# Attention softmax transposed on VectorE in 32x32 blocks and exchanged by DMA, the value product placed behind the next scores

## The reference

```python
x = _rmsnorm(hidden_states, ln_weight)
h_q = (x @ w_q.T).reshape(b, lq, H, DH)
h_k = (key_value_states @ w_k.T).reshape(b, lk, H, DH)
h_v = (key_value_states @ w_v.T).reshape(b, lk, H, DH)
score = jnp.einsum('bqhd,bkhd->bhqk', h_q, h_k)
score = score + position_bias[None]
score = jnp.where(m, score, -jnp.inf)
score = jax.nn.softmax(score, axis=-1)
score = jnp.where(m, score, 0.0)
attn = jnp.einsum('bhqk,bkhd->bqhd', score, h_v).reshape(b, lq, H * DH)
out = attn @ w_out.T
return hidden_states + out
```

## Time and profile before

| what | value |
|---|---|
| median of three runs | 943.55 us |
| the profiled execution, first to last instruction | 942.7 us |
| PE busy | 933.8 us, 99% |
| PE weight loading busy | 816.1 us, 87% |
| DVE busy | 629.9 us, 67% |
| ACT busy | 409.5 us, 43% |
| POOL busy | 520.2 us, 55% |
| DMA, mean of 16 engines | 51.6% of the span, 182 GB/s |
| TensorE clock granted | 1.00 of full speed |

### The profile page before, as it was taken

The page is one execution under the profiler, slowest core; times in us unless marked ns, Lnnn a source line. Parts: engine busy times, 40 slices in busy tenths (PEclk is TensorE's granted clock), DMA queues, the critical chain, the costliest instruction groups (busy, mean ns, idle before and its releaser), DMA issues.

```text
span 942.7 us, 16961 instructions
## 1 busy us (share of the span) xinstructions
PE 933.8 (99%) x5517; PEld 816.1 (87%) x5517; DVE 629.9 (67%) x1161; ACT 409.5 (43%) x1143; POOL 520.2 (55%) x582
## 2 busy tenths in 40 slices
PE   9999999999999999999999999999999999999997
PEld 7888898888888888888888888988898888878885
DVE  5666664466766576756766676657665767886787
ACT  5664434344343434333434344334434344335664
POOL 3450724457565756584757565856567553133477
PEclk9999999999999999999999999999999999999999
DMA  9315327674667365745676376637673666230101
GB/s 329 110 55 177 121 116 267 215 254 153 227 228 264 119 256 197 280 150 207 221 268 204 137 268 240 212 133 279 217 271 133 224 207 224 69 123 1 35 23 68
DMA packets 61291, 171.70 MB, mean 182 GB/s; under 512 B 6056, under 2 KB 8492, under 8 KB 60989
## 3 DMA queue, kind: packets, MB, share of 16 engines
q1 hardware_dynamic: 61244, 171.11, 51.6%
HBM read 159.56 MB, written 11.53 MB: 181 GB/s over the span
## 4 chain that ended last, share of the span: by engine, by line
PE 94%; DVE 2%; ACT 1%; issue 1%; POOL 1%; DMA 1%; SPq 0%; ACTq 0%; DVEq 0%; POOLq 0%
PE ps_q L355 7%; PE ps_q L357 7%; PE ps_q L356 7%; PE ps_o L355 6%; PE ps_o L357 6%; PE ps_o L356 6%; PE ps_k L355 6%; PE ps_k L357 6%; PE ps_v L355 6%; PE ps_k L356 6%; PE ps_v L357 6%; PE ps_t L2183 6%; PE ps_v L356 6%; PE ps_s L2156 6%; PE ps_t L2173 3%
## 5 line engine op out<-in xcount | busy, mean ns | idle before, releaser
L780 ACT ACTIVATE scores<-scores,neg_max 128x128 f32<-128x128 f32 x256 | 99.8, 391 | 219.9 <-DVE neg_max L1583 219.8
L1470 DVE TENSOR_TENSOR acc<-ps_o,acc 128x512 f32<-128x512 f32 x128 | 87.8, 686 | 60.9 <-PE ps_o L357 60.9
L355 PE MATMUL ps_o<-wo_hi,att_hi 128*128 128x512 f32 x256 | 105.9, 414 | 0.0
L357 PE MATMUL ps_o<-wo_hi,att_lo 128*128 128x512 f32 x256 | 100.3, 392 | 0.0
L356 PE MATMUL ps_o<-wo_lo,att_hi 128*128 128x512 f32 x256 | 100.0, 390 | 0.0
L786 ACT COPY probs_t<-ps_t 128x512 f32<-128x512 f32 x64 | 37.7, 588 | 139.5 <-PE ps_t L2173 139.4
L1104 POOL TENSOR_TENSOR shift<-bias_sb,mask_sb 128x512 f32<-128x512 f32 x64 | 84.8, 1326 | 2.9 <-DVE scores L1579 2.9
L1458 DVE TENSOR_TENSOR att_lo<-ps_t,att_hi 128x512 fp32r<-128x512 f32 x64 | 44.2, 691 | 55.2 <-ACT att_hi L773 55.2
L1145 POOL TENSOR_TENSOR wq_lo<-raw_q,wq_hi 128x256 fp32r<-128x256 f32 x65 | 48.1, 740 | 58.9 <-ACT wq_hi L612 58.9
L355 PE MATMUL ps_v<-wv_hi,ct_hi 128*128 128x256 f32 x264 | 75.1, 284 | 0.4 <-POOL wv_lo L1125 0.3
L357 PE MATMUL ps_v<-wv_hi,ct_lo 128*128 128x256 f32 x264 | 74.7, 283 | 0.0
(11 more groups left out here) (394 smaller groups left out, 2780.9 us busy)
## 6 DMA issues: line engine op xcount, KB each, us to landing
ring_hi<-scratch_x_t SPq DMA_DIRECT2D x39, 512.0 KB, 4.0
ring_lo<-scratch_x_t SPq DMA_DIRECT2D x39, 512.0 KB, 4.9
ring_hi<-scratch_c_t SPq DMA_DIRECT2D x39, 512.0 KB, 4.0
ring_lo<-scratch_c_t SPq DMA_DIRECT2D x39, 512.0 KB, 5.3
raw_o<-in_w_o SPq DMA_DIRECT2D x16, 512.0 KB, 4.9
raw_q<-in_w_q SPq DMA_DIRECT2D x15, 512.0 KB, 6.4
raw_k<-in_w_k SPq DMA_DIRECT2D x15, 512.0 KB, 7.1
xt_hi<-scratch_x_t SPq DMA_DIRECT2D x13, 512.0 KB, 7.3
```

The source lines that it names most:

```text
L355: pe.matmul(dst, hi_l, hi_r, start=first, stop=False)
L357: return pe.matmul(dst, lo_l, hi_r, start=False, stop=last)
L780: e = act.activation(probs[n][:, m, :], scores[n][:, m, :], ACT.Exp, bias=neg_max[:, n, m:m + 1], accum_out=row_sum[:, n, m:m + 1])
L1470: dve.tensor_tensor(acc[:, b, :], ps_o[:], acc[:, b, :], ALU.add).then_inc(o_added, 1)
```

## The change

The transposition leaves PE. Where a score tile is q by k, DVE now writes the sum of score and bias in another order: column k = 4r + j of tile m goes to place (j, m, r). Exponentials and division work on this order. Then one DVE instruction transposes all 32x32 blocks of the 128x512 tile in place. After it, partition 32i + r holds for each j and m the 32 query rows of block i at key 4r + j. Four DMAs, issued by ACT (pt_exchange), bring these to probs_t: DMA i takes 32 partitions with four pieces of 512 bytes each and writes 128 partitions, one piece to each. PE reads probs_t as four runs of 32 columns for a product with the values. The last step, 63, keeps the old way over PE and ACT.

The value product of a step moves behind the scores of the next step, and the split into low part moves on DVE behind the next softmax_front. The number of projection units between the value product and output part 0 becomes two; for that, one unit moves ahead of output part 0 in c = 0, 1, 2 and 3. The exponentials no longer wait for the transposes of two steps before; softmax_front waits until the exchange of two steps before has landed.

```diff
+Q = 32
...
+        def by_block(tile):
+
+            return tile[:].rearrange("p a b -> p (a b)").rearrange("p (j m r) -> p j m r", j=4, m=4)
+
+        def flat(tile):
+            return tile[:].rearrange("p a b -> p (a b)")
...
+        pt_in, PT_ALL = pt_out, 64 * (STEPS - 1)
...
             def exponentials(s, n):
 
                 act.wait_ge(s_neg, s + 1)
-                wait_from(act, pt_done, s - 1)
                 for m in range(4):
-                    e = act.activation(probs[n][:, m, :], scores[n][:, m, :], ACT.Exp,
+                    tile = scores[n][:, m, :] if isinstance(s, int) and s == STEPS - 1 else by_block(scores[n])[:, :, m, :]
+                    e = act.activation(tile, tile, ACT.Exp,
                                        bias=neg_max[:, n, m:m + 1], accum_out=row_sum[:, n, m:m + 1])
                 e.then_inc(e_done, 1)
 
+            def pt_exchange(s, n):
+
+
+
+                act.wait_ge(p_done, s + 1)
+                for i in range(4):
+                    act.dma_start(probs_t[:, i, :], scores[n][i * Q:(i + 1) * Q, :, :]).then_inc(pt_in, 16)
+
             def pt_evac(s):
-                act.wait_ge(pt_done, s + 1)
+                act.wait_ge(pt_done, 1)
...
-                pt_evac(s)
+                pt_exchange(s, n)
...
-                dve.tensor_tensor(scores[n][:], blocks(ps_s), shift[n][:], ALU.add).then_inc(s_shifted, 1)
-                dve.wait_ge(s_shifted, s + 1)
-                dve.tensor_reduce(row_max[:, n, :], scores[n][:], AX_X, ALU.max).then_inc(s_chain, 1)
-                dve.wait_ge(s_chain, 3 * s + 1)
+                wait_from(dve, pt_in, 64 * (s - 1))
+                if isinstance(s, int) and s == STEPS - 1:
+                    dve.tensor_tensor(scores[n][:], blocks(ps_s), shift[n][:], ALU.add).then_inc(s_shifted, 1)
+                    dve.wait_ge(s_shifted, s + 1)
+                    dve.tensor_reduce(row_max[:, n, :], scores[n][:], AX_X, ALU.max).then_inc(s_chain, 1)
+                else:
+                    dve.tensor_tensor(by_block(scores[n]).rearrange("p j m r -> p m r j"),
+                                      ps_s[:].rearrange("p (m r j) -> p m r j", m=4, j=4),
+                                      shift[n][:].rearrange("p m (r j) -> p m r j", j=4), ALU.add).then_inc(s_shifted, 1)
+                    dve.wait_ge(s_shifted, s + 1)
+                    dve.tensor_reduce(row_max[:, n, :], by_block(scores[n]).rearrange("p j m r -> p m j r"), AX_XY,
+                                      ALU.max).then_inc(s_chain, 1)
+                dve.wait_ge(s_chain, 4 * s + 1)
                 dve.tensor_scalar(neg_max[:, n, :], row_max[:, n, :], -1.0, None, ALU.mult).then_inc(s_neg, 1)
 
             def softmax_back(s, n):
                 dve.wait_ge(e_done, s + 1)
                 dve.reciprocal(row_inv[:, n, :], row_sum[:, n, :]).then_inc(s_chain, 1)
-                dve.wait_ge(s_chain, 3 * s + 2)
+                dve.wait_ge(s_chain, 4 * s + 2)
                 dve.scalar_tensor_tensor(row_fac[:, n, :], row_max[:, n, :], -MASKED / 3.0, row_inv[:, n, :],
                                          ALU.is_gt, ALU.mult).then_inc(s_chain, 1)
-                dve.wait_ge(s_chain, 3 * s + 3)
-                dve.tensor_tensor(probs[n][:], probs[n][:], row_fac[:, n, :].unsqueeze(2).broadcast_to([P, 4, P]),
-                                  ALU.mult).then_inc(p_done, 1)
+                dve.wait_ge(s_chain, 4 * s + 3)
+                if isinstance(s, int) and s == STEPS - 1:
+                    dve.tensor_tensor(probs[n][:], probs[n][:], row_fac[:, n, :].unsqueeze(2).broadcast_to([P, 4, P]),
+                                      ALU.mult).then_inc(p_done, 1)
+                else:
+                    dve.tensor_tensor(by_block(probs[n]), by_block(probs[n]),
+                                      row_fac[:, n, :].unsqueeze(1).unsqueeze(3).broadcast_to([P, 4, 4, Q]),
+                                      ALU.mult).then_inc(s_chain, 1)
+                    dve.wait_ge(s_chain, 4 * s + 4)
+                    dve.transpose(flat(probs[n]), flat(probs[n])).then_inc(p_done, 1)
 
             def step_first(s):
                 n = s % 2
+                softmax_front(s, n)
                 if s > 0:
                     attention_rest(s - 1)
-                softmax_front(s, n)
...
-                attention_rest(s - 1)
...
                 softmax_front(s, n)
+                attention_rest(s - 1)
...
-                pe.wait_ge(pt_out, s + 1)
+                whole = isinstance(s, int) and s == STEPS - 1
+                if whole:
+                    pe.wait_ge(pt_out, PT_ALL + 1)
+                else:
+                    pe.wait_ge(pt_in, 64 * (s + 1))
+                    wait_from(pe, att_lo_s, s)
                 pe.wait_ge(v_out, made)
                 n = c // 2 if not isinstance(s, int) or s >= FIRST else c // 2 % 2
                 for j in range(2):
                     for h in range(2):
                         m = 2 * j + h
+                        moving = probs_t[:, m, :] if whole else flat(probs_t).rearrange("p (i m c) -> p i m c", i=4, m=4)[:, :, m, :]
                         last = pe.matmul(ps_t[:, m * P:(m + 1) * P], vv[n][:, 2 * (c % 2) + j, h * P:(h + 1) * P],
-                                         probs_t[:, m, :], start=True, stop=True)
+                                         moving, start=True, stop=True)
                 last.then_inc(pv_done, 1)
...
             pe.wait_ge(q_out, 2)
             project_q(2, 2, first_use=True)
-            step_transpose(0, 0)
             pe.wait_ge(v_out, 3)
             project_v(3, 3)
+
+            step_scores(1, 1)
             step_values(0, 0, 2)
-
-            step_scores(1, 1)
             plain_q(3, 3)
             output(0, 0, 0, (0,))
             plain_k(4, 4)
-            step_transpose(1, 1)
             output(0, 0, None, (1,))
-            step_values(1, 1, 2)
...
             for s in range(2, FIRST):
                 c = s % LOOP_STEPS
                 step_scores(s, c)
+                step_values(s - 1, c - 1, s + 1 - (s - 1) % 2)
                 plain_q(s + 2, (s + 2) % LOOP_STEPS)
                 output(s - 1, (s - 1) % LOOP_STEPS, 1 if s == 5 else None, (0,))
                 plain_k(s + 3, (s + 3) % LOOP_STEPS)
                 step_v(s + 2, s + 2, (s + 2) // 4)
-                step_transpose(s, c)
                 output(s - 1, (s - 1) % LOOP_STEPS, None, (1,))
-                step_values(s, c, s + 2 - s % 2)
...
                 step_scores(s, c)
+                if c == 0:
+                    step_values(s - 1, 7, v_count(i - 1, 14))
+                elif static and s <= 4 * PLAIN:
+                    step_values(s - 1, c - 1, s - 1 - (c - 1) % 2 + 2)
+                elif not own:
+                    step_values(s - 1, c - 1, 16)
+                else:
+                    step_values(s - 1, c - 1, v_count(i, (1, 2, 11, 12, 13, 14, 14)[c - 1]))
                 if c == 6 and coming:
                     v_p6(i + 1, 1)
                 if c == 7 and coming:
@@ -2413,18 +2456,24 @@
                     q_p4(G)
                 if last and c == 5:
                     k_p3(g)
-                output(s - 1, (c - 1) % LOOP_STEPS, g if c % 4 == 1 else None, (0,))
-                if c % 4 == 0:
+                if c == 0:
                     k_p5(g)
                 if c % 4 == 1 and more:
                     q_p6(G)
+                if c == 2:
+                    q_p2(G)
+                if c == 3:
+                    k_p4(G)
+                output(s - 1, (c - 1) % LOOP_STEPS, g if c % 4 == 1 else None, (0,))
...
-                if c % 4 == 2:
+                if c == 6:
                     q_p2(G)
-                if c % 4 == 3:
+                if c == 7:
                     k_p4(G)
...
-                step_transpose(s, c)
                 output(s - 1, (c - 1) % LOOP_STEPS, None, (1,))
-                if static and s < 4 * PLAIN:
-                    step_values(s, c, s - c % 2 + 2)
-                elif not own:
-                    step_values(s, c, 16)
-                else:
-                    step_values(s, c, v_count(i, (1, 2, 11, 12, 13, 14, 14, 14)[c]))
```

26 lines of the change are left out of this document (14 added, 12 removed).

## The result

| | before | after |
|---|---|---|
| median of the runs (range) | 944.47 us (943.39 to 945.53) | 1099.98 us (1099.64 to 1106.27) |
| the profiled execution, first to last instruction | 942.7 us | 1098.1 us |

The change makes the kernel slower by a sixth: the ratio is 1.1666, 95% interval 1.1635 to 1.1697. The forecast was 959 us, and the measured time lies far above its range of 918 to 980.

A forecast was written before the change was run, and what follows sets the result against it. PE, busy 933.8 of 942.7 us, was taken as the bound. 942.7 less 27.7 for transposes plus 43 of waits gave 958.0, plus 0.85 for the runs' median: 959 us, slower by 1.6%, range 918 to 980.

The forecast's parts named there:

- 17 late steps: Steps whose values come late to PE, some 17 in all; any added softmax time there was taken as lost.
- 43 us of waits: PE waiting for the exchange: 29 us in c = 7, 6 in c = 3, 8 at the two ends.
- Moving the value product ... changes PE's order but not its work: nothing.: On PE, values behind the next scores and one projection unit ahead of output part 0 cost 0 us.
- if PE waits for att_lo, my reading of the moved units fails: Sign against the forecast: PE waiting for att_lo or a projection's buffer instead of the exchange; no size given.
- In the other steps DVE waits there for the exponentials: Outside c = 3 and 7, DVE's wait hides the moved att_lo additions, which delay the reciprocal 0.60 us.
- the room up to the next scores: Time from exchange issue to the next scores' end on PE: 2.76 us in c = 7, 4.26 in c = 3.
- 27.7 us taken from PE: Transposes leaving PE in 63 steps, 0.44 us a step, counted as a gain of 27.7 us.
- By turns: Likeliest case, 0.45: engines alternate ACT's and SP's pieces; c = 7 exchange 7.6 us, wait 4.8; total 945 to 972.
- The fixed part: Exchange time beyond moving its pieces, taken from a small store: 1.6 us, beside 6.0 for 32 pieces per engine.
- the rival in which the exchange waits behind all that SP has issued: Exchange lands only after SP's issued loads: c = 7 waits 7.0 us, 978 us in all; chance 0.10.
- The last one leaves about 1.2 us after the first: ACT's four DMA issues, spaced as SP's 0.43 us; the last leaves about 1.2 us after the first.
- The scattered write: DVE's sum with bias, each element 512 bytes apart: taken at 0; by the skill's rule 0.5 us, 8 in all.

The follow-up runs named there:

- order_alone: Kernel before with only PE's and DVE's new order, moved units and last two steps included; transposes stay on PE, ACT's order stays: 975.43 us.
- order_and_turn: order_alone plus DVE's 32x32 transposition ahead of the signal that the probabilities are done; PE still makes its own transposes: 995.47 us.
- no_dma_wait: Changed kernel without the four exchange DMAs; ACT still waits for the transposed tile, PE reads that tile in place: 990.07 us.
- order_k_copy: order_alone with ACT's key copy put ahead of its high part of the attention result in c = 2 and c = 6: 954.06 us.
- v_high_first: Changed kernel with ACT's key copy ahead of att_hi, plus ACT's copies into wv_hi ahead of the exchange in c = 5, 6 and 7: 1063.32 us.
- plain_write: Changed kernel with scores, exponentials and division in the old contiguous column order; transposition and exchange stay: 1102.59 us.

## Why the prediction was wrong

The ledger, from the chain before, order_alone, order_and_turn, no_dma_wait, after. Each line is what a part cost with those above it in place; in another order the lines would differ.

| part | us | my sum |
|---|---|---|
| the order alone (975.4 - 944.0) | +31 | 0 |
| the transposition on DVE (995.5 - 975.4) | +20 | in 17 late steps, 12 |
| PE's transposes and ACT's copy out, scattered write in (990.1 - 995.5) | -5 | -27.7 |
| the DMAs, their waits and ACT's issuing (1100.0 - 990.1) | +110 | about 31 |

My 43 us of waits are split here: 17 late steps by 0.72 belong to the transposition. Of the 141 us between forecast and result, 79 are in the last line, 31 in the first, 23 in the third and 8 in the second. So the largest step that failed is the size of the exchange with what follows from its wait; the first one on the way is the order taken at nothing.

- **"Moving the value product ... changes PE's order but not its work: nothing."** This is the step that failed first, 31 us against 0. PE's work is the same, and order_k_copy shows that the moved units cost nothing in the turns. But I moved the values and did not follow what is queued behind them on ACT: att_hi waits for them, behind it the key copy, behind this DVE's mid and the softmax front. The sign that I had named (if PE waits for att_lo, my reading of the moved units fails) came true, for 25.4 us. I had listed ACT's queue in c = 7 alone. Of the 31 us the knot is 21; of the 10 behind the turns only the wait for mm_lo (3.7 us, with about 1.7 for the lower clock behind it) has a name.
- **"In the other steps DVE waits there for the exponentials", and the room up to the next scores.** I measured room for the softmax only against the values behind the next scores. The first addition to acc stands behind it on DVE, and output part 1 has only one unit between itself and part 0. In no_dma_wait PE waits 23.3 us for acc; in order_and_turn the list has no such wait, but 8.3 for the transposes. So of 27.7 us taken from PE, and 8.3 of waits that went with them, 29 came back as waits for acc and att_lo (23.3 + 25.5 - 19.6); what is left, 7 us, is nearly the 5 measured. The products did go (PE's busy time falls from 951.5 us in order_and_turn to 923.0 in no_dma_wait, by the 28 that I had), but from steps whose end DVE now sets.
- **The size of the exchange.** By turns, 7.6 us in c = 7; measured 9.5. The turns themselves were right: the 512 pieces, 32 for each of 16 engines, take 4.9 us, 0.15 each, where I had 0.187. The DMA records show 626 of SP's pieces between them, most of 2 KB where I had taken 4. The fixed part was wrong: 1.6 us, against 4.0 to the first piece. The rule of the Trainium skill (DMA: Bandwidth & Descriptors, Queues, rings and completion order) that rings are served in turn agrees with these counts; it does not give the 2.8 us more ahead of the first piece, and what makes them stays open. PE's wait is 6.4 to 6.9 us for the exchange of c = 7, not 4.8, and 1.4 to 2.9 for that of c = 3 (5.7 in turn 1), not 1.2; all over the span 66.3 instead of 43. In c = 7 that is close to the 7.0 of the rival in which the exchange waits behind all that SP has issued, by another mechanism: in turn 2 the first piece moves 4.0 us after the issue, and SP's raw_k, issued before it, lands after 7.4.
- **The clock.** Each of the six waits of 6.4 to 6.9 us is followed by products at the lower clock, for 3.0 to 5.2 us, so 1.5 to 2.6 us are lost each time (half of it). With it c = 0 is 8.7 us longer. I had no term for it; the kernel before has no such stretch to read it from.
- **"The last one leaves about 1.2 us after the first"**: 1.9 after, and ACT is held for 2.5. Behind the issues stand ACT's copies for POOL; PE waits 13.3 us for wv_lo. The prediction gives ACT's issuing no price. v_high_first shows that 2.8 us a turn hang on it.
- **The scattered write.** Taken at 0, it takes 0.38 more. The rule of the Trainium skill (Advanced Engine Details and Errata, Memory Cachelines), a penalty for a different line at each access, is borne out in kind; the 8 us that I had worked out beside it are not, since plain_write gained nothing.
- **Right**: 0.71 us for the transposition, four entries left in the transposes' group, waits in every eighth and, smaller, every fourth step, an exchange under 5 us in the median and above 6 in c = 7 (2.3 and 7.0 by the issues). The values' four runs of 32 columns cost nothing: in c = 6 the next product starts 0.81 us after them, and before it was 0.89.

What stays open: of the 155 us, the 6 ahead of step 8, the 16 of turn 1 and the 30 from step 56 on were not taken apart as turns 2 to 6 were, and the share of the 110 us that follows from ACT's issuing was measured in c = 5 and 6 only.
